# Attention with the mask added by TensorE, a plain maximum on VectorE, and value products in pairs of key groups

## The reference, cut to what matters

```python
q = (x @ q_w + q_b) / math.sqrt(HEAD)          # 16 heads of 8, batch 4, 1024 tokens
k = x @ k_w + k_b
v = x @ v_w + v_b
scores = jnp.einsum('bhqd,bhkd->bhqk', q, k)
causal = jnp.tril(jnp.ones((s, s), bool))
scores = jnp.where(causal, scores, neg)
attn = jax.nn.softmax(scores, axis=-1)
ctx = jnp.einsum('bhqk,bhkd->bhqd', attn, v)
```

## Time and profile before

| | |
|---|---|
| runs, us | 2724.48 median of 3 (2720.82 to 2725.66) |
| profiled execution | 2722.04 us, span 2720.3 |
| steady attention, first layer | 157 to 694 us of the span |
| steady attention, second layer | 1824 to 2363 us |
| maxima alone ahead of them | 26 us each |

### The profile page before, as it was taken

How to read it: one execution, slowest core, us unless ns; L and a number is a source line. 1 busy time by engine, 2 the same in 40 slices (tenths; PEclk the granted TensorE clock), 3 DMA queues, 4 the chain that set the end, 5 groups by cost and what they waited for, 6 DMA issues and landing times. The chain is left out here.

```text
span 2720.3 us, 46007 instructions
## 1 busy us (share of the span) xinstructions
PE 1840.4 (68%) x10834; PEld 1030.2 (38%) x10928; DVE 1686.4 (62%) x5324; ACT 951.4 (35%) x1988; POOL 945.0 (35%) x1548
## 2 busy tenths in 40 slices
PE   3399889899611971469990065469899899840593
PEld 1133333333510760269990043223333333340473
DVE  6588778887341225767773485678788788452223
ACT  2246556566300320000000032236566566610231
POOL 4012222222455440058770472102222222337342
PEclk8689999999755995689995588669999999955797
DMA  2511111010002435000003001311111101001344
GB/s 69 173 62 26 27 27 25 22 25 8 1 28 68 132 99 140 0 0 0 0 0 39 16 8 47 89 47 26 27 25 24 27 18 22 2 0 50 103 140 127
DMA packets 109188, 120.12 MB, mean 44 GB/s; under 512 B 31264, under 2 KB 71584, under 8 KB 107936
## 3 DMA queue, kind: packets, MB, share of 16 engines
q1 hardware_dynamic: 92448, 96.50, 13.8%
q0 software_dynamic: 8192, 16.86, 1.8%
q10 hardware_dynamic: 8320, 4.19, 0.6%
HBM read 71.01 MB, written 45.71 MB: 43 GB/s over the span
## 5 line engine op out<-in xcount | busy, mean ns | idle before, releaser
L719 DVE CUSTOM_DVE_ANT_0 pA<-pA,causal 128x512 f32<-128x512 f32 (+3 forms) x1536 | 824.0, 583 | 183.7 <-PE pA L562 167.2
L763 ACT ACTIVATE wt<-pB 128x512 f32<-128x512 f32 (+3 forms) x1536 | 654.4, 496 | 443.2 <-PE pB L603 290.1
L804 POOL TENSOR_SCALAR_AFFINE_SELECT wt<-wt 128x128 f32<-128x128 f32 x1024 | 290.3, 293 | 769.2 <-ACT wt L763 748.6
L562 PE MATMUL pA<-ka,qa 125*128 125x512 bf16 (+3 forms) x1536 | 487.8, 344 | 70.6 <-PEq L258 30.0
L603 PE MATMUL pB<-qa,ka 128*128 128x512 bf16 (+3 forms) x1442 | 429.2, 334 | 52.8 <-issue 24.2
L619 PE MATMUL pC<-wt,va 128*32 128x512 f32 (+3 forms) x3072 | 346.4, 497 | 0.1
L603 PEld LDWEIGHTS pB<-qa,ka 128*128 128x128 bf16 x1536 | 145.5, 98 | 421.0 <-ACT wt L763 255.8
L562 PEld LDWEIGHTS pA<-ka,qa 125*128 125x128 bf16 x1536 | 147.9, 98 | 248.4 <-DVE mx L719 162.8
L719 DVE DVE_READ_ACCUMULATOR2_ANT mx<- 128x1 f32 x1536 | 217.5, 142 | 0.0
L1195 POOL DMA_INDIRECT y<-eo,dest x128 | 122.5, 957 | 184.5 <-issue 112.4
L1057 POOL DMA_INDIRECT xin<-keep_v,keep_send x128 | 126.9, 991 | 82.6 <-DVE keep_send L1030 43.8
(11 more groups left out here) (236 smaller groups left out, 2512.2 us busy)
## 6 DMA issues: line engine op xcount, KB each, us to landing
w<-in_L_ffn_fc_w_dram SPq DMA_DIRECT2D x64, 256.0 KB, 3.2
qa<-qk_parts SPq DMA_DIRECT2D x192, 64.0 KB
ka<-qk_parts SPq DMA_DIRECT2D x192, 64.0 KB
xi<-xin SPq DMA_DIRECT2D x32, 258.0 KB, 3.6
qk_parts<-qp SPq DMA_DIRECT2D x24, 256.0 KB, 2.4
qk_parts<-kp SPq DMA_DIRECT2D x24, 256.0 KB, 2.8
xin<-zero SPq DMA_DIRECT2D x4, 1032.0 KB, 7.1
y<-zero SPq DMA_DIRECT2D x4, 1024.0 KB, 12.6
```

The source lines that it names most:

```text
L562: pe.matmul(slot(s, n)[:, 0:b - a], qa[s.stage][0:MROW, h, i * P:(i + 1) * P], ka[s.stage][0:MROW, h, a:b], start=True, stop=True).then_in ...
L719: vec.tensor_tensor_reduce(out=slot(s, n)[:, 0:size], in0=slot(s, n)[:, 0:size], in1=mask, scale=1.0, scalar=LOWEST, op0=ALU.add, op1=ALU.max,
L763: act.activation(wt[g % NW][h][:, 0:e - a], pB[(g * GH + h) % NB][:, 0:e - a], ACT.Exp).then_inc(exp_done, 1)
L804: pool.affine_select(out=block_, in_=block_, compare_op=ALU.is_ge, fill=0.0, base=0, pattern=[[1, P]], channel_multiplier=-1).then_inc(mas ...
```

## The change

The mask of a piece that ends on the diagonal is added by a second matmul into the same PSUM bank, of the bf16 identity with a bf16 128x128 tile `future` that holds the lowest value above the diagonal. VectorE takes `reduce_max` of the piece, without write-back and without accumulator read. Products are issued after every second group, for two groups at once, with LAG = 3 and NW = 4; groups 10 and 11 keep blocks of their own at the end of a step. The rule for pieces counts the columns of both groups of a pair, with LEAD as before.

```diff
--- before.py
+++ after.py
@@ -118,7 +118,7 @@
     for name in ("ident", "upper", "ones"):
         c[name] = core.sb(ctx, name, [P, P])
     c["ident_b"] = core.sb(ctx, "ident_b", [P, P], BF16)
-    c["causal"] = core.sb(ctx, "causal", [P, SEQ])
+    c["future"] = core.sb(ctx, "future", [P, P], BF16)
     c["rev"] = core.sb(ctx, "rev_expert", [P, E])
     c["num"] = core.sb(ctx, "expert_number", [P, E])
     c["spill"] = core.sb(ctx, "spill_row", [P, TILES])
@@ -176,8 +176,8 @@
             chain.link(pool.affine_select(out=c["upper"][:, :], in_=c["upper"][:, :], compare_op=ALU.is_ge, fill=0.0,
                                           base=0, pattern=[[1, P]], channel_multiplier=-1))
 
-            chain.link(pool.memset(c["causal"][:, :], 0.0))
-            chain.link(pool.affine_select(out=c["causal"][:, SEQ - P:], in_=c["causal"][:, SEQ - P:],
+            chain.link(pool.memset(c["future"][:, :], 0.0))
+            chain.link(pool.affine_select(out=c["future"][:, :], in_=c["future"][:, :],
                                           compare_op=ALU.is_ge, fill=LOWEST,
                                           base=0, pattern=[[-1, P]], channel_multiplier=1))
             pool.iota(c["rev"][:, :], pattern=[[-1, E]], base=E, channel_multiplier=0,
@@ -477,7 +477,7 @@
     LINKS_LO, LINKS_HI, LINKS_CTX = 3, 4, 2
     NA, NB = 3, 3
     LEAD = 0.6
-    NW, LAG = 3, 2
+    NW, LAG = 4, 3
     NLINK = LINKS_LO + LINKS_HI + LINKS_CTX
     with ExitStack() as ctx:
         sb = lambda n, s, dt=F32: core.sb(ctx, n + tag, s, dt)
@@ -559,8 +559,13 @@
                     if e == 0:
                         pe.wait_ge(qk_loaded[s.stage], s.fills * 32 * TERMS + 32 * TERMS)
                     reached(pe, a_used, event(s, n) - (NA - 1))
-                    pe.matmul(slot(s, n)[:, 0:b - a], qa[s.stage][0:MROW, h, i * P:(i + 1) * P],
-                              ka[s.stage][0:MROW, h, a:b], start=True, stop=True).then_inc(a_done, 1)
+                    diagonal = b == (i + 1) * P
+                    last = pe.matmul(slot(s, n)[:, 0:b - a], qa[s.stage][0:MROW, h, i * P:(i + 1) * P],
+                                     ka[s.stage][0:MROW, h, a:b], start=True, stop=not diagonal)
+                    if diagonal:
+                        last = pe.matmul(slot(s, n)[:, b - a - P:b - a], c["ident_b"][:, :], c["future"][:, :],
+                                         start=False, stop=True)
+                    last.then_inc(a_done, 1)
 
                 def maxima(s, n, half, count):
 
@@ -630,17 +635,18 @@
                     total = 2 * sum(e - a for j, a, e in GROUP)
                     passed = n = 0
                     for g, (j, a, e) in enumerate(GROUP):
-                        behind = GROUP[g - LAG][2] - GROUP[g - LAG][1] if g >= LAG else 0
+                        pair = (g - LAG, g - LAG + 1) if g >= LAG and g % 2 else ()
+                        behind = sum(GROUP[k][2] - GROUP[k][1] for k in pair)
                         for h in range(GH):
                             scores(s, g, h)
                             passed += (e - a) / GH + (behind * LEAD if h == GH - 1 else 0)
                             while n < count and sum(share[:n + 1]) <= sum(share) * passed / total:
                                 run(s, n)
                                 n += 1
-                        if g >= LAG:
-                            products(s, g - LAG)
-                            passed += behind * (1 - LEAD)
-                    for g in range(NG - LAG, NG):
+                        for k in pair:
+                            products(s, k)
+                        passed += behind * (1 - LEAD)
+                    for g in range(NG - LAG + 1, NG):
                         passed += GROUP[g][2] - GROUP[g][1]
                         while n < count and sum(share[:n + 1]) <= sum(share) * passed / total:
                             run(s, n)
@@ -713,12 +719,8 @@
                             context(s, n, 0, n_lo + 2)
                         else:
                             h, i, a, b = PIECE[e]
-                            size = b - a
-                            mask = c["causal"][:, SEQ - size:] if b == (i + 1) * P else c["causal"][:, 0:size]
                             apart(vec, a_done, event(s, n) + 1)
-                            vec.tensor_tensor_reduce(out=slot(s, n)[:, 0:size], in0=slot(s, n)[:, 0:size], in1=mask,
-                                                     scale=1.0, scalar=LOWEST, op0=ALU.add, op1=ALU.max,
-                                                     accum_out=mx[a // HALF][:, i, h:h + 1]).then_inc(a_used, 1)
+                            vec.reduce_max(mx[a // HALF][:, i, h:h + 1], slot(s, n)[:, 0:b - a], AX).then_inc(a_used, 1)
 
                             if 0 <= e <= 3 and n_lo:
                                 if e == 0:
```

## The result

The changed kernel takes 2804.1 us (median of 4 runs, 2799.7 to 2817.9) against 2725.1 for the kernel before in the same runs: a ratio of 1.031, 95% interval 1.0285 to 1.0331. It is 79 us slower; the forecast was 36. The profiled execution is the slowest of the four, 2817.9 us with a span of 2816.2; it alone has a trace, so what it has over the median stays open.

The account below looks back on a forecast made before the run. Attention was taken as bound by two full engines, TensorE and VectorE, stopping each other through few buffers. 30 steps by +1.4 us gave +42, starts -2, last units -2: +38 us, forecast 2760 us, range 2690 to 2805.

Parts of the forecast that it names:

- the relief of 2.0 us a step: VectorE's maxima: 0.04 us less for each of 48 pieces a step, bounds 0 and 3.4 us.
- Masks: Second matmul on 32 diagonal pieces a step: 0.06 us each, +1.9 us on TensorE's path, bounds 1.8 and 3.1.
- Joined blocks: TensorE products: 12 blocks become 7, five joints of about 0.2 us save 1.0 us a step.
- the -0.5 for GpSimd's masks: Later product blocks find weights already masked by GpSimd; of 1 us waited a step, 0.5 counted as saved.
- The order: Bunched scores, pieces and products in a step run queues dry: 35.4 us against 34.03, +1.4 us with net work.
- Stretches 2 and 3: Step parts of groups 4, 5 and 6, 7: forecast 6.0 us from 5.81 and 6.2 us from 6.19.
- the wait at MAX_HI: Groups 10 and 11: TensorE stands from 0.6 to 1.4 us for the split before the upper maxima's transposes.
- now fill a wait for ScalarE (-0.4): First stretch, groups 0 to 3: group 3's four scores fill a ScalarE wait, -0.4 us, giving 7.6 from 7.89.
- The ends: Two starting units of maxima, -2 us in all; two last units gain five joints, -2 us in all.
- What would show it: Signs in the first layer's steady stretch: ScalarE waits above 127 us, VectorE waits below 65, GpSimd's masks not waited for.
- set the pace: Rival: VectorE's relief comes back one for one, 2660 us, or 2690 at half; chance 0.30.
- Dear masks: Rival: mask weight loads uncovered, 0.10 us each, 1.3 us more a step, 2800 us; chance 0.12.

Follow-up runs that it names:

- max_no_mask: Kernel before with the plain maximum and no mask in the maxima, old product order: 2696.7 us, 0.988 of the kernel before.
- mask_only: Changed kernel with the old product loop, NW 3 and LAG 2, keeping mask matmuls and plain maximum: 2719.5 us, 0.9985 of the kernel before.
- tail_joined: Old order with masks and plain maximum, products of groups 10 and 11 joined behind the last pieces: 2723.7 us, 1.0000 of the kernel before.
- lag3_single: Changed kernel with NW 4 and LAG 3 but a single product block after every group: 2747.5 us, 1.008 of the kernel before.
- pairs_lag2: Changed kernel with LAG 2, the same pairs joined behind groups 2, 4, 6, 8 and 10: 2752.3 us, 1.0105 of the kernel before.
- split_67: Changed kernel with only the pair of groups 6 and 7 split, as blocks behind groups 8 and 9: 2756.1 us, 1.011 of the kernel before.
- last_single: Changed kernel with single product blocks at lag 2 in the last unit of each layer alone: 2795.3 us, 1.027 of the kernel before.
- pairs_only: Kernel before with the new paired loop, NW 4 and LAG 3, mask and maximum still on VectorE: 2824.9 us, 1.036 of the kernel before.

## Why the prediction was right in sign and short in size

- **VectorE: right.** 686 ns and a start-to-start of 0.6 us were foretold from the earlier trace rows; the relief of 2.0 us a step (48 times 0.04 is 1.9) came out as 2.2 (70 us over 32 units). The Trainium skill (VectorE: DVE Perf Modes, Rules for kernel authors) calls `tensor_reduce` the slowest VectorE operation. The trace does not agree for this exchange: 686 ns against 716, and max_no_mask is 27 us faster than before.
- **Masks: price right, weight too high.** 0.06 us each, as was said, the loads hidden (masks at 407.45 and 407.62 in the changed kernel, the next piece 0.06 us behind each). But the sum laid all of 1.9 us a step on the path; measured, 23 us in the old order, 0.8 a step. Relief and masks came through at some 0.4 of their work each, as the first part argued of two full engines, and cancelled (mask_only -4 us). The sum used that for VectorE's relief and not for the masks, and so by luck made up for some of what the order had too low.
- **Joined blocks: seen in the trace, not in the time.** The block of 512 + 512 lasts 1.86 us to the next matmul against two of 1.00, 0.14 saved there and more at the entry. The term of -1.0 us a step counted it as time; tail_joined gives none that shows. Nor did the -0.5 for GpSimd's masks come: the loads still wait 16.1 us for them, 17.1 before.
- **The order: the step that failed, by its size.** It was forecast as 35.4 us a step, and "30 steps by 1.4". The undisturbed step measured 36.16, so +2.1, by the other steps +2.3: some 25 us short over 30 steps. Stretches 2 and 3 were right (6.01, 6.24 for 6.0, 6.2), the fifth nearly (5.96 for 6.1), with the wait at MAX_HI that was named (TensorE idle 0.79 for 0.8). The first was 8.05, not 7.6, the fourth 7.01, not 6.8, the tail 2.89, not 2.7. In the first, "now fill a wait for ScalarE (-0.4)" did not happen: the last scores still wait for ScalarE, and the block takes 1.44 us:

```profile
348.75 0.28 PE L608 MATMUL pB<-qa,ka 128*128 128x256 bf16 x1 [0.21 <-ACT wt L765]
...
350.12 1.28 PE L624 MATMUL pC<-wt,va 128*32 128x512 f32 x16
351.56 0.49 PE L563 MATMUL pA<-ka,qa 125*128 125x512 bf16 x2 [0.16 <-issue]
```

  lag3_single, pairs_lag2 and split_67 confirm the reason given, bunched work that leaves ScalarE and VectorE dry, and put 85 us on it (changed kernel less mask_only, the last units and the clock included) where the forecast had 30 steps by 1.0, the 1.4 less 0.4 of net work.
- **One step stood for thirty: wrong.** The two last steps of a layer lost 3.1 and 3.5, 2.0 over the common loss in each layer. That the unit at 612.6 took 31.9 us before was read as speaking for a rival; it lost more than the others did.
- **The ends: wrong sign for the last units.** -1 each was forecast for five joints; they grew by 3.0 and 3.4, some 2 of each by the order and the rest by the clock, and by the trace last_single gives 4.7 back. The starts were right (-1.7 for -1 in the first layer).
- **The clock: not foreseen**, 6 us in the steps and some 2 in the last units.
- **What remains.** Per layer the forecast was -1 + 21 - 1 = +19, measured -1.7 + 42.4 + 3.7 = +44.4, 88.6 with the second in the profiled execution. Its other 7 us lie in stages whose code is the same, and they scatter: the first piece began at 128.0 to 136.7 us over the kernels' profiles. The change does not explain them.
- **What would show it.** Waits for VectorE fell below 65 us as said (40.7). Waits for ScalarE were to rise above 127 and fell to 103.3: with fewer but longer stops, the loss shows on the engines that wait for TensorE (VectorE 141, ScalarE 149.5), and that was the wrong sign to look for. GpSimd was to be waited for no longer; it is, 16.1 us for 17.1.
- **Rivals.** VectorE does not set the pace: 70 us of relief gave 27 in the old order and 34 under pairs. Dear masks hit the size (2800) by a wrong mechanism.

What stays open is how the 24 us that lag 3 and joining cost only together divide among the waits. split_67 points at one block, with VectorE's wide pieces before it and MAX_HI behind it, but a hand-over moved there moves all others too.

## What to carry to other kernels

Where two engines are nearly full and feed each other through a few buffers, the order in which work is handed over can cost more than the work it saves: a joint that saved some 0.1 to 0.2 us of TensorE time went with idle times of 1.8 us on VectorE and 3.9 us on ScalarE (2.7 before). Before joining blocks, list what each neighbour has queued for the length of the joined block and what waits on it right behind; a long block belongs behind work that another engine must finish, not ahead of it. And price a change of order on every kind of step (first, looped, unrolled, last), not on one.

## What the runs showed of the hardware that was not expected

- The granted clock fell to 0.50 for short stretches of the steady work. Inside steps this came with the joined block of groups 6 and 7: four in the profiled execution of the changed kernel, ten without masks, eleven in pairs_only. What came before is alike: 128-wide pieces 0.6 us apart (0.65 in pairs_only, below), each waiting for VectorE:

```profile
598.45 0.23 PE L562 MATMUL pA<-ka,qa 125*128 125x128 bf16 x1 [0.43 <-DVE mx L720]
599.10 0.23 PE L562 MATMUL pA<-ka,qa 125*128 125x128 bf16 x1 [0.42 <-DVE mx L720]
599.26 3.53 PE L619 MATMUL pC<-wt,va 128*32 128x512 f32 x16
```

  The block is not needed for it. In the last unit of the changed kernel the clock fell 1.5 us before the first block, and in the kernel before it falls behind the starts of loop turns, three in each layer. In their steps split_67, with blocks of 8 products there, and pairs_lag2, with 16 but other pieces before them, have it at loop turns alone. What exactly decides it was not tried apart.
- A maximum read from PSUM costs what one from SBUF does, 686 ns at 512 columns.
- A second matmul into the same bank, with 128 new weight columns, costs 0.06 us where its load (100 ns) is hidden.
